# Layer 0 window attention: blocks of 64 queries or keys in two column halves of the array, one bank a head, and a step's value products in one place

## The chip, the cores and the metric

The kernel runs on one core of a Trainium2 chip. The metric is the device time of one execution in microseconds. Three runs of the kernel before took 5398.77 to 5411.32 us, with a median of 5408.9 us.

## The reference, cut to what matters

The program is a two-layer model over 16 sequences of 512 tokens with 256 features. The change touches only the attention of layer 0, in which each query sees its own key and the 64 keys before it, in 16 heads of 16 features:

```python
offsets = jnp.arange(-W, 1)[None, :]                  # W = 64
idx = q_pos + offsets
local_mask = (idx < 0) | (idx >= S_k)
k_win = k[:, :, gidx, :];  v_win = v[:, :, gidx, :]
scores = jnp.einsum('bhqd,bhqwd->bhqw', q, k_win)
scores = jnp.where(mask, -jnp.inf, scores)
m = jnp.max(scores, axis=-1, keepdims=True)
e = jnp.exp(scores - m)
probs = e / jnp.sum(e, axis=-1, keepdims=True)
ctx = jnp.einsum('bhqw,bhqwd->bhqd', probs, v_win)
```

Everything after it (the gate, the full attention of layer 1, the experts) is the same in both kernels.

## The kernel before, in words

The program is a row of stages with a barrier of all engines between them: `project_context`, `window_attention`, `close_window`, `open_full`, `full_attention`, `close_full`, `route`, `experts`. The change is in `window_attention` and in the mask constants of `shape_constants`.

`window_attention` makes 64 steps, one for each sequence and group of four heads. Queries and keys lie in SBUF as stacks of 96 rows of bf16 (`qst`, `kst`, three parts of each number), with three more rows for the shift, that is the negated maximum of a query. A step has two kinds of products:

- *Items* find the maximum. Queries lie on the output's partitions, keys on its columns. In the kernel before an item is one head and two blocks of 128 queries (`MAXJOBS`, eight a step). One matmul of the identity with the constant `outside` (384 columns of bf16) fills the bank with 0 or a large negative number (L789), and two products of 192 or 128 columns are added to it (L794). VectorE takes the maximum along the columns (L754). After the last item of a step it makes the shift in five small operations in a chain, each of which waits for the one before (L759 to L763). The shift is turned by TensorE (the *turn*, L783), copied by VectorE (L749), and sent into row 96 of the query stack by a DMA that ScalarE issues (`send_shift`, L713).
- *Scores* are computed again with keys on the partitions, now with the shift (L805 for the mask, L808 for the products). A head takes two banks, and two heads have their banks at a time. ScalarE takes the exponential of a head in one instruction, 128 partitions by 768 elements (L728). *Values* then multiply the exponentials by the values and a column of ones, in fp32: for each of four blocks of keys the four heads go to partitions 0, 32, 64 and 96 of one bank (L821). ScalarE copies the bank to SBUF (L709), and SyncE stores it (L658).

The order is written out by hand. In window `s`, TensorE does scores of head 0, the first value block of step `s-1`, two items of step `s+3`; scores of head 1, value block 1, the turn of step `s+2` and an item; scores of head 2, value block 2, two items; scores of head 3, value block 3, three items. The turn of step `s+2` needs the chain of small operations behind the last item of step `s+2`, which is the last item of window `s-1`. The items go through three banks in turn. On VectorE the items stand in the same order. ScalarE has the four exponentials, `send_shift` behind the second of them, and the copy of the values at the end. GpSimd places the values of step `s+1` into the padded tile `vaug` once the value products of step `s-1` are done. SyncE loads the stacks five steps ahead (three DMAs for keys, six for queries), and stores the result of the step before. A prologue makes the items of steps 0, 1 and 2 and the turns of steps 0 and 1.

Of the kernel before, what the change touches and what calls it, by code (L numbers as in the profile page):

```python
# [7 lines left out]
ACT = mybir.ActivationFunctionType  # L8
# [545 lines left out]
def window_attention(nc, d):  # L554
# [4 lines left out]
    HQ = GROUP * QT  # L559
    SPAN = P + WINDOW  # L560
# [9 lines left out]
    def window_items(s, left):  # L570
# [9 lines left out]
        at = len(prologue) + PER_WINDOW * (s.k % 3)  # L580
        return [(*it, base + n, (at + n) % 3) for n, it in enumerate(items)]
# [10 lines left out]
    prologue = [(*it, n, n % 3) for n, it in enumerate(prologue)]  # L592
    assert PER_WINDOW % 3 == 0

    with ExitStack() as ctx:
        sp_ = Space(nc, ctx, "win")
        sb, ps = sp_.sb, sp_.ps
        score = [ps(f"score{i}", [P, 2, 512]) for i in range(2)]
        item_bank = [ps(f"item{i}", [P, 512]) for i in range(3)]
        value = ps("value", [P, SQ])  # L600
# [4 lines left out]
        prob = [[sb(f"prob{h}{i}", [P, 2, 2 * SPAN]) for i in range(2)] for h in range(GROUP)]  # L605
# [7 lines left out]
        outside = sb("outside", [P, 2, 2 * SPAN], BF16)  # L613
# [9 lines left out]
        place_start, vaug_done = sem("place_start"), sem("vaug_done")  # L623
# [58 lines left out]
        def _(pool):  # L682
# [4 lines left out]
            pool.wait_ge(pads_set, 4)  # L687

# [16 lines left out]
        def _(act):  # L705
            def read_values(s):
                act.wait_ge(value_done, s.n + 1)
                at_least(act, attn_out[s.par], 16 * half(s))
                nc.scalar.copy(raw[s.par][:, :], value[:, :]).then_inc(value_read, 1)  # L709

# [8 lines left out]
            act.wait_ge(ones_in, 32 * STACKS)  # L719
            for k in range(2):  # L720
                send_shift(Eighth(0, k))

            def window(s, first, left):
                for h in range(GROUP):
# [3 lines left out]
                    nc.scalar.activation(prob[h][s.par][:, :, :], score[h % 2][:, :, 0:2 * SPAN], ACT.Exp,  # L728
# [6 lines left out]
            read_values(Eighth(0, STEPS - 1))  # L735

        @block.vector
        def _(dve):
# [4 lines left out]
            def item(kind, s, j, number, bank):  # L743
                dve.wait_ge(item_full, number + 1)
                if kind == "turn":
# [3 lines left out]
                    nc.vector.tensor_copy(shiftT[s.par][:, :], item_bank[bank][:, :].bitcast(BF16)[:, 0:P]).then_inc(item_read, 1)  # L749
                    return  # L750
                h, qts = MAXJOBS[j]
                hq = h * QT + qts[0]
# [12 lines left out]

            for it in prologue:
                item(*it)

            def window(s, first, left):
                for it in window_items(s, left):  # L770
                    item(*it)
# [2018 lines left out]
```

## Time and profile before

| | |
|---|---|
| runs shown | 5398.77, 5408.9, 5411.32 us |
| profiled execution | 5409.27 us, span 5407.4 us |
| busy share of the span | PE 90%, DVE 72%, ACT 50%, POOL 23% |
| granted TensorE clock, mean | 0.941 |
| items' maxima, L754 | 512 instructions, mean 552 ns, 262.0 us busy |
| exponentials of the scores, L728 | 256 instructions, mean 811 ns, 207.5 us busy |

Times are microseconds from the start of the span. PE is TensorE's matmuls, PEld its weight loads, DVE VectorE, ACT ScalarE, POOL GpSimd, SP SyncE; a q behind an engine is its sequencer. A busy matmul row runs from its start until its last result has landed, so rows that follow each other overlap, and the distance of two starts is what one costs in a stream. The stage of the change runs from about 328.7 us to 825.8 us of the span. The clock is given as a share of 2.4 GHz.

### The profile page before, as it was taken

To read this page: it belongs to the slowest core of one execution; us is meant where nothing else is said; L and a number is where in the kernel's file an instruction comes from. 1 tells how busy PE (TensorE), PEld (TensorE's weight loads), DVE (VectorE), ACT (ScalarE), POOL (GpSimd) and SP (SyncE) were. 2 spreads that over 40 slices of the span, in tenths; PEclk is the share of its full clock that TensorE was granted. 3 is DMA by queue.
4 is the path that set the end of the run, shared out by engine and by line. 5 is a ranking of instruction groups with operands and counts; after the bars stand their busy time and mean duration, and the time that the engine had idled before them with its cause. 6 is when DMAs were issued, how large, how long until landed. Compare 5 with 4: busy or idle time off the path is not lost. (4 is left out here: it accounts for less than half of the span.)

```text
span 5407.4 us, 90976 instructions
## 1 busy us (share of the span) xinstructions
PE 4887.9 (90%) x28783; PEld 2800.2 (52%) x28784; DVE 3896.2 (72%) x7609; ACT 2692.4 (50%) x3563; POOL 1236.4 (23%) x964
## 2 busy tenths in 40 slices
PE   8979997997699999999999999999997911999999
PEld 4546665775244444443444444444432710888887
DVE  7766765664768888887888878888884831787786
ACT  2225552222337777776677767777764100444443
POOL 5620001222611010010010001000000345454454
PEclk9989998998889999999999999999998855999999
DMA  7765654223843323323323333323221654333332
GB/s 218 222 179 163 163 143 120 82 69 100 255 88 74 66 47 69 67 59 75 66 46 72 67 60 74 62 49 71 51 45 49 199 157 157 60 61 81 60 61 36
DMA packets 326812, 519.64 MB, mean 96 GB/s; under 512 B 50000, under 2 KB 242863, under 8 KB 324192
## 3 DMA queue, kind: packets, MB, share of 16 engines
q1 hardware_dynamic: 294816, 461.48, 35.0%
q0 software_dynamic: 28208, 51.82, 4.6%
q8 instruction: 226, 3.70, 0.3%
q14 instruction: 202, 1.65, 0.1%
q10 hardware_dynamic: 3360, 0.98, 0.1%
HBM read 254.97 MB, written 179.55 MB: 80 GB/s over the span
## 5 line engine op out<-in xcount | busy, mean ns | idle before, releaser
L1185 DVE TENSOR_REDUCE full_peak<-full_item 128x1 f32<-128x512 f32 (+2 forms) x3392 | 2035.3, 654 | 467.1 <-PE full_item L1252 461.6
L1155 ACT ACTIVATE full_prob<-full_score 128x1024 f32<-128x1024 f32 (+1 forms) x1792 | 1650.8, 961 | 641.4 <-PE full_score L1263 634.4
L1252 PE MATMUL full_item<-full_kst,full_qst 49*128 49x512 f32 (+1 forms) x4096 | 1204.1, 406 | 36.7 <-DVE full_peak L1185 24.3
L1263 PE MATMUL full_score<-full_qst,full_kst 51*128 51x512 f32 (+1 forms) x3328 | 1110.8, 448 | 21.2 <-ACT full_prob L1155 12.1
L1263 PEld LDWEIGHTS full_score<-full_qst,full_kst 51*128 51x128 f32 (+1 forms) x3328 | 480.5, 183 | 935.9 <-ACT full_prob L1155 602.3
L1277 PE MATMUL full_value<-full_prob,full_vaug 128*17 128x512 f32 x6656 | 886.5, 605 | 0.8 <-ACT full_raw L1142 0.7
L1252 PEld LDWEIGHTS full_item<-full_kst,full_qst 49*128 49x128 f32 x4096 | 630.7, 189 | 180.2 <-DVE full_peak L1185 129.8
L2562 ACT ACTIVATE moe_h<-moe_hbank,moe_b 128x512 f32<-128x512 f32 (+1 forms) x320 | 199.9, 625 | 453.8 <-PE moe_hbank L2655 447.8
L1100 POOL TENSOR_TENSOR full_low<-full_low,full_high 128x1601 f32<-128x1601 f32 x32 | 115.7, 3615 | 1194.3 <-DVE full_high L1171 1194.3
L2665 PE MATMUL moe_ybank<-moe_w_both,moe_h_high 128*128 128x512 f32 x1088 | 386.5, 399 | 0.0
L1096 POOL TENSOR_TENSOR full_low<-full_low,full_keep 128x1601 f32<-128x1601 f32 x32 | 116.0, 3624 | 1068.1 <-ACT full_low L1128 1068.1
L754 DVE TENSOR_REDUCE win_peak<-win_item 128x2 f32<-128x384 f32 x512 | 262.0, 552 | 124.0 <-PE win_item L794 117.1
L728 ACT ACTIVATE win_prob<-win_score 128x768 f32<-128x768 f32 x256 | 207.5, 811 | 266.5 <-PE win_score L808 263.3
L2667 PE MATMUL moe_ybank<-moe_w_both,moe_h_low 128*128 128x256 f32 x1088 | 304.6, 280 | 0.0
L2527 POOL DMA_INDIRECT out<-moe_y,moe_to_token x136 | 234.5, 1724 | 121.7 <-POOL moe_y L2523 86.9
L2653 PE MATMUL moe_hbank<-moe_x_high,moe_w_high 128*128 128x512 f32 (+1 forms) x640 | 236.6, 370 | 17.7 <-DVE moe_x_low L2593 15.7
L1277 PEld LDWEIGHTS full_value<-full_prob,full_vaug 128*17 128x17 f32 x6656 | 110.4, 95 | 246.9 <-issue 223.8
L2523 POOL TENSOR_SCALAR moe_y<-moe_y,moe_weight 128x256 f32<-128x256 f32 x136 | 194.6, 1431 | 190.8 <-issue 110.6
L2655 PE MATMUL moe_hbank<-moe_x_high,moe_w_low 128*128 128x512 f32 (+1 forms) x640 | 236.3, 369 | 0.0
L2654 PE MATMUL moe_hbank<-moe_x_low,moe_w_high 128*128 128x512 f32 (+1 forms) x640 | 235.9, 369 | 0.0
L2665 PEld LDWEIGHTS moe_ybank<-moe_w_both,moe_h_high 128*128 128x128 f32 x1088 | 204.2, 188 | 47.1
L1227 PE MATMUL full_score<-full_ctxT,full_wk 128*128 128x512 f32 (+1 forms) x512 | 218.5, 552 | 4.6 <-DMA full_ctxT<-in_ctxT 3.6
(274 smaller groups left out, 7197.3 us busy)
## 6 DMA issues: line engine op xcount, KB each, us to landing
full_kst<-full_high SPq DMA_DIRECT2D x256, 200.1 KB
full_ctxT<-in_ctxT SPq DMA_DIRECT2D x16, 1601.0 KB, 9.0
full_kst<-full_low SPq DMA_DIRECT2D x128, 200.1 KB
win_qst<-scratch_q SPq DMA_DIRECT2D x384, 64.0 KB, 2.7
full_qst<-scratch_q SPq DMA_DIRECT2D x384, 64.0 KB
scratch_xbuf<-ctxp_zero POOLq DMA_DIRECT2D x17, 1032.0 KB, 7.8
moe_x<-scratch_xbuf SPq DMA_DIRECT2D x32, 516.0 KB, 3.7
scratch_attn<-win_raw SPq DMA_DIRECT2D x64, 256.0 KB, 2.1
```

The costliest lines, as they stand in the source:

```text
L754: nc.vector.tensor_reduce(peak[s.par][:, hq:hq + 2], src, AX, ALU.max).then_inc(item_read, 1)
L1155: nc.scalar.activation(prob[h][(s.par * PAIRS + t) % 2][0:rows, 0:banks, :], score[u % 2][0:rows, 0:banks, :], ACT.Exp, scale=SCALE).then_ ...
L1185: nc.vector.tensor_reduce(peak[s.par][:, hq:hq + len(qts), c], src, AX, ALU.max).then_inc(item_read, 1)
L1252: ins = nc.tensor.matmul(ps[:, at:at + z - a], qst[s.slot][rows, h // 2, qt * P:(qt + 1) * P].bitcast(F32R), kst[s.slot][rows, h // 2, a:z ...
L1263: ins = nc.tensor.matmul(score[u % 2][0:z - a, kt % 2, :], kst[s.slot][rows, h // 2, a:z].bitcast(F32R), qst[s.slot][rows, h // 2, :].bitc ...
L1277: ins = nc.tensor.matmul(value[32 * h:32 * h + VW, :], vaug[batch_par(s)][0:rows, kt, GROUP * s.slot + h, :], src, start=(kt == 0), stop=( ...
L2527: pool.indirect_dma_start(d["out"], bass.IndirectOffsetOnAxis(to_token[pg][:, i:i + 1], 0), y[pg][:, i, :], None, bounds_check=TOKENS + SL ...
L2653: nc.tensor.matmul(out, high, x_high[pg][:, kc, 0:cols], start=(kc == 0), stop=False)
L2654: nc.tensor.matmul(out, high, x_low[pg][:, kc, 0:cols], start=False, stop=False)
L2655: ins = nc.tensor.matmul(out, low, x_high[pg][:, kc, 0:cols], start=False, stop=(kc == KC - 1))
L2665: nc.tensor.matmul(bank[:, :, :], h_high[:, hc, i * P:(i + 1) * P], w2_both[par][:, hc, :, :], start=(hc == 0), stop=False, skip_group_che ...
L2667: ins = nc.tensor.matmul(bank[:, 0, :], h_low[:, hc, i * P:(i + 1) * P], w2_both[par][:, hc, 0, :], start=False, stop=(hc == HC - 1), skip ...
```

## The change

Scores and items work on blocks of 64. An item is now one head (four a step instead of eight), in one bank of 128 partitions by 4 by 128 columns: the queries of a block of 64 lie in the lower or the upper 64 partitions and see 128 keys. Each product has 64 columns of weights and goes to partitions 0 to 63 or 64 to 127, so that the mask takes two matmuls of 512 columns and the head eight products of 128 columns. Scores have the same form, and a head takes one bank instead of two. The exponential of a head takes two ScalarE instructions, one for each half of the partitions, 512 elements each, which write to different columns of a tile `prob` that GpSimd has cleared at the start of the stage (ScalarE waits for this, `prob_set`). There are four item banks instead of three, and two value banks instead of one. All four value blocks of step `s-1` stand in one place, behind the items of head 1. One item instead of two stands ahead of the turn (`AHEAD`). VectorE instead of ScalarE copies the value bank; the copy stands behind the third of the four items.

```diff
-    MAXJOBS = [(h, [qt, qt + 1]) for h in range(GROUP) for qt in (0, 2)]
     UNITS = GROUP
-    NMAX = len(MAXJOBS)
+    NMAX = GROUP
     PER_WINDOW = NMAX + 1
-    AHEAD = 2
+    ITEM_BANKS = 4
+    AHEAD = 1
...
-        score = [ps(f"score{i}", [P, 2, 512]) for i in range(2)]
-        item_bank = [ps(f"item{i}", [P, 512]) for i in range(3)]
-        value = ps("value", [P, SQ])
+        score = [ps(f"score{i}", [P, kts, P]) for i in range(2)]
+        item_bank = [ps(f"item{i}", [P, QT, P]) for i in range(ITEM_BANKS)]
+        value = [ps(f"value{i}", [P, SQ]) for i in range(2)]
...
+            for i in range(2):
+                for h in range(GROUP):
+                    nc.gpsimd.memset(prob[h][i][:, :, :], 0.0).then_inc(prob_set, 1)
...
             act.wait_ge(ones_in, 32 * STACKS)
+            act.wait_ge(prob_set, 2 * GROUP)
...
-                    nc.scalar.activation(prob[h][s.par][:, :, :], score[h % 2][:, :, 0:2 * SPAN], ACT.Exp,
+                    nc.scalar.activation(prob[h][s.par][0:HALF, :, 0:P], score[h % 2][0:HALF, :, :], ACT.Exp, scale=SCALE)
+                    nc.scalar.activation(prob[h][s.par][HALF:P, :, HALF:SPAN], score[h % 2][HALF:P, :, :], ACT.Exp,
                                          scale=SCALE).then_inc(exp_done, 1)
...
-                if not first:
-                    read_values(s.plus(-1))
...
-                nc.vector.tensor_reduce(peak[s.par][:, hq:hq + 2], src, AX, ALU.max).then_inc(item_read, 1)
+                nc.vector.tensor_reduce(peak[s.par][:, j * QT:(j + 1) * QT], item_bank[bank][:, :, :], AX,
+                                        ALU.max).then_inc(item_read, 1)
...
+                nc.vector.tensor_copy(raw[s.par][:, :], value[s.par][:, :]).then_inc(value_read, 1)
+
             def window(s, first, left):
-                for it in window_items(s, left):
+                items = window_items(s, left)
+                for it in items[:4]:
+                    item(*it)
+                if not first:
+                    read_values(s.plus(-1))
+                for it in items[4:]:
                     item(*it)
...
+            def mask(bank, which):
+
+                for half_row in range(2):
+                    m = slice(HALF * half_row, HALF * half_row + HALF)
+                    nc.tensor.matmul(bank[m, :, :].rearrange("p i k -> p (i k)"), ident16[:, m], outside[:, which, :],
+                                     start=True, stop=True)
...
+                mask(ps, 0)
+                for qt in range(QT):
+                    for half_row in range(2):
+                        q = qt * P + half_row * HALF
+                        a, z = max(0, q - WINDOW), q + HALF
+                        ins = nc.tensor.matmul(ps[half_row * HALF:(half_row + 1) * HALF, qt, P - (z - a):P],
+                                               qst[s.slot][0:SHIFT_ROW, j, q:q + HALF], kst[s.slot][0:SHIFT_ROW, j, a:z],
+                                               start=False, stop=True, skip_group_check=True)
                 ins.then_inc(item_full, 1)
...
+                mask(ps, 1)
                 for kt in range(kts):
+                    for half_row in range(2):
+                        k = kt * P + half_row * HALF
+                        z = min(k + P, SQ)
+                        ins = nc.tensor.matmul(ps[half_row * HALF:(half_row + 1) * HALF, kt, 0:z - k],
+                                               kst[s.slot][:, h, k:k + HALF], qst[s.slot][:, h, k:z],
+                                               start=False, stop=True, skip_group_check=True)
                 ins.then_inc(score_full, 1)
...
+            def values(s):
+
+                pe.wait_ge(vaug_done, s.n + 1)
+                at_least(pe, value_read, s.n - 1)
+                pe.wait_ge(exp_done, UNITS * s.n + UNITS)
+                for kt in range(kts):
+                    for h in range(GROUP):
+                        a, z = kt * P, min(kt * P + SPAN, SQ)
+                        ins = nc.tensor.matmul(value[s.par][32 * h:32 * h + 32, a:z], vaug[s.par][:, kt, h, :],
+                                               prob[h][s.par][:, kt, 0:z - a],
+                                               start=(kt == 0), stop=True, skip_group_check=True)
+                ins.then_inc(value_done, 1)
...
+            ITEMS_AFTER = (2, 1, 1, 1)
+            VALUES_AFTER = 1
...
                 for h in range(GROUP):
                     scores(s, h)
-                    if not first:
-                        values(s.plus(-1), h)
-                    due = len(items) * (h + 1) // GROUP
-                    for it in items[given:due]:
+                    for it in items[given:given + ITEMS_AFTER[h]]:
                         item(*it)
-                    given = due
+                    given += ITEMS_AFTER[h]
+                    if h == VALUES_AFTER and not first:
+                        values(s.plus(-1))
```

So a window of TensorE reads: scores 0, item 0, turn; scores 1, item 1, the values of the step before; scores 2, item 2; scores 3, item 3. VectorE has: item 0, the copy of the turn, items 1 and 2, the copy of the values, item 3 with the chain of small operations.

## Rows read from the trace of the kernel before

**Rows 1.** Busy time in stretches; columns: stretch, length, five engines, clock, DMA share, GB/s.
```profile
342.30:360.30 18.00, 13.82 (x74) 9.08 (x74) 14.37 (x35) 0.00 (x0) 0.74 (x2) 0.69 1.06 208
365.00:800.00 435.00, 435.00 (x4823) 274.07 (x4820) 305.32 (x837) 221.43 (x298) 23.75 (x59) 1.00 0.59 160
```

**Rows 2.** One step in order of time; columns: start, us, engine, line, what.
```profile
500.44 0.23 PE L783 MATMUL win_item<-win_ident,win_shift_parts 128*128 128x128 bf16 x1
...
500.50 0.33 PE L789 MATMUL win_item<-win_outside,win_ident 128*128 128x384 bf16 x1
500.50 0.26 PEld L794 LDWEIGHTS win_item<-win_kst,win_qst 96*128 96x128 bf16 x2
500.66 0.30 PE L794 MATMUL win_item<-win_kst,win_qst 96*128 96x128 bf16 x2
...
500.81 0.33 PE L805 MATMUL win_score<-win_outside,win_ident 128*128 128x384 bf16 x1
...
500.96 0.73 ACTq L713 DMA_DIRECT2D win_qst<-win_shiftT  x1
...
501.00 0.56 DVE L754 TENSOR_REDUCE win_peak<-win_item 128x2 f32<-128x384 f32 x1
...
501.30 0.30 PE L808 MATMUL win_score<-win_qst,win_kst 99*128 99x192 bf16 x2
501.53 0.16 PEld L821 LDWEIGHTS win_value<-win_prob,win_vaug 128*32 128x32 f32 x8
501.53 0.53 PE L821 MATMUL win_value<-win_prob,win_vaug 128*32 128x192 f32 x8
...
502.00 0.34 PE L789 MATMUL win_item<-win_outside,win_ident 128*128 128x384 bf16 x1
...
504.27 1.49 DVE L754 TENSOR_REDUCE win_peak<-win_item 128x2 f32<-128x384 f32 x3 [0.71 <-PE win_item L794]
...
506.63 0.17 DVE L763 TENSOR_TENSOR win_shift_parts<-win_shift_rest,win_shift_parts 128x16 bf16<-128x16 f32 x1
...
507.74 0.23 PE L783 MATMUL win_item<-win_ident,win_shift_parts 128*128 128x128 bf16 x1
```

**Rows 3.** Groups by shape, whole span; behind the bar: busy us, mean ns.
```profile
L1263 PEld LDWEIGHTS full_score<-full_qst,full_kst 51*128 51x128 f32 x3072 | 448.3, 187 | 812.0 <-ACT full_prob L1155 478.5 <-issue 318.3
...
L1277 PEld LDWEIGHTS full_value<-full_prob,full_vaug 128*17 128x17 f32 x6144 | 101.9, 95 | 222.2 <-issue 200.2 <-ACT full_prob L1155 15.0 <-ACT full_vaug L1132 5.5
```

**Rows 4.** The last value products and the pause before them, in order of time.
```profile
823.75 1.40 PE L821 MATMUL win_value<-win_prob,win_vaug 128*32 128x192 f32 x32 [1.07 <-ACT win_raw L709]
```

**Rows 5.** Groups of VectorE and ScalarE by shape, whole span, columns as in rows 3.
```profile
L1185 DVE TENSOR_REDUCE full_peak<-full_item 128x1 f32<-128x512 f32 x3072 | 1944.3, 684 | 396.5 <-PE full_item L1252 391.1
...
L2588 DVE TENSOR_SCALAR moe_x_cut<-moe_tbank 128x512 uint32<-128x512 uint32 x64 | 41.0, 681 | 0.0
...
L416 DVE SCALAR_TENSOR_TENSOR ctxp_turned<-ctxp_bank,ctxp_bk,ctxp_cos 128x512 f32<-128x512 f32 x32 | 23.8, 742 | 2.0 <-PE ctxp_bank L478 2.0
...
L1155 ACT ACTIVATE full_prob<-full_score 65x512 f32<-65x512 f32 x256 | 142.4, 591 | 64.8 <-PE full_score L1263 63.5
```

**Rows 6.** The first turn in order of time, behind an idle TensorE.
```profile
348.77 0.17 DVE L763 TENSOR_TENSOR win_shift_parts<-win_shift_rest,win_shift_parts 128x16 bf16<-128x16 f32 x1
...
349.09 0.22 PE L783 MATMUL win_item<-win_ident,win_shift_parts 128*128 128x128 bf16 x1 [1.78 <-DVE win_shift_parts L763]
```

**Rows 7.** SyncE's loads in a step, in order of time.
```profile
498.34 1.26 SPq L647 DMA_DIRECT2D win_kst<-scratch_k  x3
499.70 2.86 SPq L652 DMA_DIRECT2D win_qst<-scratch_q  x6
```

**Rows 8.** Stretches around pauses of TensorE, columns as in rows 1.
```profile
347.10:350.50 3.40, 1.04 (x9) 0.61 (x8) 2.01 (x9) 0.00 (x0) 0.00 (x0) 1.00 1.04 207
350.60:353.90 3.30, 3.30 (x18) 2.22 (x17) 3.08 (x7) 0.00 (x0) 0.00 (x0) 0.50 1.07 216
...
822.10:825.00 2.90, 1.83 (x43) 1.30 (x41) 0.00 (x0) 1.29 (x2) 0.00 (x0) 1.00 0.17 64
```

More of the change, by code:

```diff
@@ L579, in window_items @@
         base = len(prologue) + PER_WINDOW * s.n
-        at = len(prologue) + PER_WINDOW * (s.k % 3)
-        return [(*it, base + n, (at + n) % 3) for n, it in enumerate(items)]
+        at = len(prologue) + PER_WINDOW * s.k
+        return [(*it, base + n, (at + n) % ITEM_BANKS) for n, it in enumerate(items)]
     def turn_number(s):
@@ L591, in window_attention @@
                 + [("max", Eighth(0, 2), j) for j in range(NMAX)])
-    prologue = [(*it, n, n % 3) for n, it in enumerate(prologue)]
-    assert PER_WINDOW % 3 == 0
+    prologue = [(*it, n, n % ITEM_BANKS) for n, it in enumerate(prologue)]
     with ExitStack() as ctx:
@@ L604, in window_attention @@
         vaug = [sb(f"vaug{i}", [P, kts, GROUP, 32]) for i in range(2)]
-        prob = [[sb(f"prob{h}{i}", [P, 2, 2 * SPAN]) for i in range(2)] for h in range(GROUP)]
+        prob = [[sb(f"prob{h}{i}", [P, kts, SPAN]) for i in range(2)] for h in range(GROUP)]
         peak = [sb(f"peak{i}", [P, HQ]) for i in range(2)]
@@ L612, in window_attention @@
         ident16 = sb("ident16", [P, P], BF16)
-        outside = sb("outside", [P, 2, 2 * SPAN], BF16)
+        outside = sb("outside", [P, 2, 4 * P], BF16)
         sem, sems = sp_.sem, sp_.sems
@@ L705, in _ @@
         def _(act):
[L706 to L709, printed above, removed]
             def send_shift(s):
@@ L810, in scores @@
-                ins.then_inc(score_full, 1)
-            def values(s, kt):
-                if kt == 0:
-                    pe.wait_ge(vaug_done, s.n + 1)
-                    at_least(pe, value_read, s.n)
-                    pe.wait_ge(exp_done, UNITS * s.n + UNITS)
-                for h in range(GROUP):
-                    a, z = kt * P, min(kt * P + SPAN, SQ)
-                    src = prob[h][s.par][:, kt // 2, kt % 2 * SPAN:kt % 2 * SPAN + z - a]
-                    ins = nc.tensor.matmul(value[32 * h:32 * h + 32, a:z], vaug[s.par][:, kt, h, :], src,
-                                           start=(kt == 0), stop=True, skip_group_check=True)
-                if kt == kts - 1:
-                    ins.then_inc(value_done, 1)
+                    for half_row in range(2):
[4 more added lines that the diff above has]
+                                               start=False, stop=True, skip_group_check=True)
@@ L834, in window @@
                     scores(s, h)
[L835 to L838 removed]
+                    for it in items[given:given + ITEMS_AFTER[h]]:
                         item(*it)
[L840 removed]
+                    given += ITEMS_AFTER[h]
+                    if h == VALUES_AFTER and not first:
+                        values(s.plus(-1))
             windows_by_eight(pe, window)
[L842 to L843 removed]
+            values(Eighth(0, STEPS - 1))
 def full_attention(nc, d):
@@ L2699, in shape_constants @@
     sin = np.stack([np.sin(ang[:, f % half]) * (-1 if f < half else 1) for f in row]).astype(np.float32)
-    r, c = np.arange(P)[:, None], np.arange(P + WINDOW)[None, :]
     bf16 = mybir.dt.np(BF16)
-    near = np.where((r <= c) & (c <= r + WINDOW), 0.0, OUTSIDE)
-    first = np.where(c < WINDOW, OUTSIDE, near)
-    outside = np.stack([np.concatenate(x, 1) for x in ((first, near), (near, near))], 1).astype(bf16)
+    r, c = np.arange(P)[:, None], np.arange(P)[None, :]
+    near = np.where((r % (P // 2) <= c) & (c <= r % (P // 2) + WINDOW), 0.0, OUTSIDE)
+    first = np.where((r < P // 2) & (c < WINDOW), OUTSIDE, near)
+    last = np.where((r >= P // 2) & (c >= WINDOW), OUTSIDE, near)
+    outside = np.stack([np.concatenate(x, 1) for x in ((first, near, near, near), (near, near, near, last))], 1).astype(bf16)
     before = (r < np.arange(P)[None, :]).astype(bf16)
```

36 lines of the change are left out of this document (10 added, 26 removed).

## The prediction

> **What bounds the kernel now.** I read the stretches first. From 365 to 800 us, nearly the whole of the stage that is changed, PE is busy 435.00 of 435.00 us at clock 1.00 (2.4 GHz), while DVE is at 305.32, ACT at 221.43 and the DMA engines at 0.59 [rows 1]. So the stage goes by TensorE, and no result of it is late. Then one step in order of time [rows 2]: the turn starts at 500.44 and the next at 507.74. The 64 turns run from 349.09 us to 808.98 us, and from the fourth on they are 7.31 us apart. In this step a mask of 384 columns takes from 500.50 to 500.66, which is 384 columns at 2.4 GHz; the two products behind it (128 and 192 columns) end their turn at 500.81. Eight such item blocks and eight score blocks are 16 x 0.32 = 5.1 us. A value block starts at 501.53 and the next work at 502.00. Of these 0.47 us the columns are only 0.32 (192 columns, two instructions a head): about 0.09 go ahead of it (products issued at 501.30 and having 320 columns are through at 501.44) and about 0.10 to 0.15 behind it. Four value blocks cost 3 x 0.47 + 0.36 and 4 x 0.09 = 2.1 us. With the turn that is 7.3 us.
>
> The chain of small operations is hidden now. The last maxima of a step are three in a row, 504.27 to 505.76; the chain ends with L763 at 506.80 [rows 2], and the turn that needs it starts at 507.74. TensorE has 2.8 us of work between the last item and the turn. This cover is what I look at below.
>
> **The change part by part.** All sums are for one step, and go against the profiled execution of 5409.3 us (span 5407.4), which lies 0.4 us from the median of 5408.9 us.
>
> *A unit (mask and products of a head).* Items and scores had 768 + 704 columns a head. Now the mask is 512 columns for each half and the products are 4 x 128 columns for each half. If the halves run side by side, the mask is 512 / 2400 = 0.22 us. Each pair of products is 128 columns, 0.053 us, and some 0.005 for an instruction. Its loads have 64 columns of bf16, a form without a row. fp32 loads have rows of 187 ns at 128 columns and 95 ns at 17 [rows 3], so 0.83 ns a column; two bf16 loads of 128 columns took 0.26 us with the wait between them (at 500.50) [rows 2], about half the fp32 ones each. 64 columns cost between 0.02 us (half of that again) and 0.053 us; I take 0.053, the dearer. That is as long as the product and so still hidden behind it. A unit u is 0.22 + 4 x 0.058 = 0.45 us. There are eight units: 3.6 us, where there were 5.1.
>
> Do the halves run side by side? The value products use four column groups of 32. The last 32 of them ran in 1.40 us [rows 4]; their columns, 2 x 4 x 704 = 5632, would take 2.35 us one after the other at one column a cycle. Eight loads of about 108 ns each began and ended within 0.16 us from 501.53 on [rows 2]; one after the other they would need 8 x 32 x 0.83 = 0.21 us and the tail of the last. So products and loads of different column groups run side by side in the form seen, with 32 columns and fp32. With 64 columns and bf16 no row shows it. The bounds are u = 0.45 (side by side) and u = 0.43 + 8 x 0.058 = 0.90 (nothing side by side); between them is u = 0.22 + 4 x 0.116 = 0.68, where only the loads follow each other. I take 0.45, since the rows of the nearest form show both kinds of overlap.
>
> The Trainium skill ("TensorE: Matmul & The Clock Gate", Part 3, "The mechanism") says that weight loads overlap running matmuls only if the row groups differ; the two halves here have the same rows. The trace differs: loads of L794 start at 500.50, while the mask L789 with the same rows runs until 500.83 [rows 2]. By that rule the loads would be laid bare, u would be near 0.66 and the step slower than before.
>
> *The values in one place.* 1.40 us from the first start to the last end [rows 4], less about 0.07 by which the next work may start ahead of that end, and 0.09 ahead: 1.42 us. Before it was 2.1. The turn now stands between products of 64-column form: 0.06 (500.44 to 500.50) [rows 2] and 0.10 to get out of it, which I take from the value blocks; bounds 0 and 0.15. Together TensorE has 3.6 + 1.42 + 0.16 = 5.2 us of work.
>
> *The chain behind the last item.* Now there are only scores 0 and item 0 between item 3 and the turn, 2u = 0.90 us. Against it stand: result of the item to VectorE 0.19 (next start at 500.81, maximum at 501.00), maximum of 512 elements 0.68 [rows 5], the chain of small operations 505.76 to 506.80, 1.05 [rows 2], and 0.15 from its end (348.94) to the turn (349.09) [rows 6]; 2.07 us. VectorE is also late, because the copy of the value bank stands between the maxima of items 2 and 3. Reading a bank with 512 elements takes 0.68 (L2588) [rows 5]; no row has a plain fp32 copy of this size by VectorE, bounds 0.56 (the maximum of 384 elements, [rows 2]) and 0.74 (another operation of 512 elements, L416 in [rows 5]). Maxima in a row are 0.08 closer than their length (three of 0.55 in 1.49) [rows 2]. So the turn of one step hangs on the turn of the step before by a ring. Turn and way out 0.16; scores 1 and item 1 0.90; values 1.42; scores 2 and item 2 0.90; to VectorE 0.19; maximum 2 0.60; copy 0.60; maximum 3 0.68; small operations 1.05; to the turn 0.15. The sum is 6.65 us, longer than TensorE's 5.2. So TensorE, now never idle, waits 1.4 to 1.5 us at each turn. The ring without the copy (over scores 3 and item 3) is 0.16 + 0.90 + 1.42 + 1.80 + 2.07 = 6.35, a lower bound. In front of the turn only head 0's work stands, so nothing else can fill this wait.
>
> *The others.* ScalarE has 8 x 0.59 (65 x 512 elements [rows 5]) and the DMA issue of 0.73 [rows 2], 5.5 us with its gaps; it loses the copy of 0.58. It stays under 6.65; without that cover it would set the step at 5.5. Exponential 1, `send_shift` and exponential 2 in a row need 1.2 + 0.8 us, and scores 2 come 2.3 us behind scores 1, so it is not late. VectorE's work is 4 x 0.68 + 0.68 + 0.23 + 1.0 = 4.6 us where it was 5.13. SyncE issues the loads in 4.2 us [rows 7], with store and registers 5.5 us, five steps ahead: hidden. The bytes are the same, and the DMA share rises from 0.59 to 0.65. The second value bank takes away a wait that is nearly nothing now. GpSimd clears eight tiles of 768 elements, 6 us by its clear of 512 elements in 0.52 us; ScalarE waits for this ahead of its first shift, which left at 349.67 us, and the clear ends at about 336 us. Hidden, 6 us if it were not.
>
> *The sum.* From 7.31 to 6.65 is 0.66 us; the steady steps are 61: 40 us. The prologue (342.3 to 360.3, [rows 1]) is held by 24 maxima and two chains, partly at the lower clock. Twelve maxima of 0.60 replace 24 of 0.47 to 0.64, about 4 us. The last two steps have no items and go by the exponentials, 4 x 1.2 us a step in both kernels: 0. Forecast 5409.3 - 44 = 5365 us; with 0.06 to 0.30 us a step for the copy and the way out of the turn its own range is 5345 to 5385.
>
> **Rivals.**
> *The weight loads of the two halves do not overlap.* Place: each pair of products; price: 0.116 instead of 0.058, u = 0.68. For it: a load of 64 columns is as long as its product, so there is no room, and no row shows two loads of 64 columns. Against it: the eight loads in 0.16 us. TensorE is then 8 x 0.68 + 1.58 = 7.0 us and waits at the turn for 2.07 - 1.36 = 0.7: 7.7 us. That is slower: 61 x 0.42 = 26, the prologue gives 3, so 5432 us. It decides from u = 0.61 on, where both the ring (4u + 4.85) and TensorE (6u + 3.65) reach 7.3. The skill's rule above would lead here too.
> *Nothing of the halves overlaps.* u = 0.90, a step of 8 x 0.90 + 1.58 + 0.3 = 9.1: 61 x 1.8 = 107, 5515 us. The change would then not do what it says. Against it are rows 4.
> *The ring does not bite*, and the step goes to 5.2 us: 61 x 2.1 + 4 = 133, 5276 us. Nothing in the order allows it, only much shorter small operations than the 0.21 us steps seen.
> *The clock falls.* A pause like the one ahead of the first turn (PE 1.04 of 3.40 us busy) was followed by clock 0.50 [rows 8]; the pause ahead of the last values (1.07 us without a result under way) was not, at 1.83 of 2.90 us busy [rows 4, 8]. A step with 5.2 of 6.65 us of work is nearer to the second. If a third of the time ran at 1.2 GHz, the ring's 3.3 us of TensorE would double there: 6.65 + 1.1 = 7.75, 5435 us.
>
> **How the numbers follow.** A measurement of this kernel tells 0.3% (16 us) from no change. Forecast 0.68; a unit of 0.55 to 0.65, which ends within 0.3%, 0.07; loads one after the other 0.11; nothing side by side 0.04; the clock 0.04; the ring not biting 0.06. Faster is 0.68 + 0.06 = 0.74, same 0.07, slower 0.19. The range from 5335 to 5433 us holds the forecast, the middle and most of the first rival; outside are 0.04 and 0.06 and the rest of the slow cases.
>
> **What would show it.** Right: maxima of 512 elements at 0.68 us, half as many; products of the lower and upper half starting within 0.01 us of each other, pairs 0.058 us apart; one value stretch of 1.4 us; turns 6.6 us apart with about 1.4 us of idle PE ahead of each, ended by the last small operation; the DVE copy directly between two maxima. Wrong: pairs 0.11 us apart, turns closer than 6.3 us, a clock under 1.00 in the steady stretch, or ScalarE or SyncE as what the turn or the scores wait for.

## The result, and the profile after

The changed kernel takes 5380.0 us (median of 5 runs, 5375.6 to 5380.8) where the kernel before takes 5406.3 us (5 runs, 5398.8 to 5411.3): a ratio of 0.9950, with a 95% interval from 0.9936 to 0.9965. That is 26 us faster, and 15 us more than the forecast of 5365. The profiled execution has a span of 5378.0 us and a time of 5379.97 us.

Two stretches of the stage, with the columns of [rows 1]: the prologue, and the steady steps.

```profile
342.30:360.30 18.00, 11.85 (x126) 8.89 (x128) 10.67 (x25) 0.00 (x0) 0.74 (x2) 0.50 1.06 216
365.00:760.00 395.00, 320.08 (x6487) 223.43 (x6483) 241.92 (x631) 272.07 (x461) 22.93 (x57) 0.97 0.63 174
```

TensorE, which had no idle time in this stage [rows 1], is now busy for 81% of it. The clock is no longer 1.00 throughout. One step in order of time, as in [rows 2]:

```profile
500.29 0.41 PE L789 MATMUL win_item<-win_outside,win_ident 128*64 128x512 bf16 x2
500.29 0.44 PEld L807 LDWEIGHTS win_item<-win_kst,win_qst 96*64 96x64 bf16 x8
500.51 0.39 PE L807 MATMUL win_item<-win_kst,win_qst 96*64 96x128 bf16 x8
...
500.73 0.38 PE L789 MATMUL win_score<-win_outside,win_ident 128*64 128x512 bf16 x2
...
500.94 0.69 DVE L749 TENSOR_REDUCE win_peak<-win_item 128x4 f32<-128x512 f32 x1 [1.62 <-PE win_item L807]
...
501.12 0.59 ACT L729 ACTIVATE win_prob<-win_score 64x512 f32<-64x512 f32 x1
...
501.55 0.68 DVE L768 COPY win_raw<-win_value 128x512 f32<-128x512 f32 x1
...
502.14 0.68 DVE L749 TENSOR_REDUCE win_peak<-win_item 128x4 f32<-128x512 f32 x1
...
503.69 0.17 DVE L759 TENSOR_TENSOR win_shift_parts<-win_shift_rest,win_shift_parts 128x16 bf16<-128x16 f32 x1
...
503.93 0.23 PE L797 MATMUL win_item<-win_ident,win_shift_parts 128*128 128x128 bf16 x1 [1.11 <-DVE win_shift_parts L759]
...
505.06 1.40 PE L833 MATMUL win_value<-win_prob,win_vaug 128*32 128x192 f32 x32
```

The reader sees the predicted step. From mask to mask (500.29 to 500.73) a unit, that is the mask and the products of one head, is 0.44 us. The masks of both halves take 0.22 of it and the eight products the other 0.22, or 0.055 us a pair: the two halves run side by side. Maximum, copy and maximum stand directly behind each other on VectorE. The last small operation starts at 503.69, and the turn that waited for it starts at 503.93, behind 1.11 us of idle TensorE. Then the values run in one piece of 1.40 us.

One sign is there that the prediction counted as wrong: the scores of head 0 wait 0.17 us for an exponential in most steps. It costs nothing, since the turn behind them waits for VectorE all the same.

Most turns are 6.55 to 6.63 us apart, where the forecast was 6.65. But ten of the intervals are longer, in pairs. The waits of TensorE's two queues between 400 and 740 us (what waited, for what; total us, times, longest) show two reasons to wait where one was foreseen:

```profile
PEld win_item L797 <- DVE win_shift_parts L759: 53.4, 42, 1.3
PEld win_score L789 <- issue: 25.6, 55, 3.3
...
PE win_score L789 <- issue: 14.7, 5, 3.1
```

"Issue" is a wait for no result of another engine. There are five long ones of some 3 us. The first in order of time:

```profile
464.27 0.39 PE L807 MATMUL win_item<-win_kst,win_qst 96*64 96x128 bf16 x8
467.70 0.64 PE L789 MATMUL win_score<-win_outside,win_ident 128*64 128x512 bf16 x2 [3.05 <-issue]
468.13 0.63 PE L820 MATMUL win_score<-win_qst,win_kst 99*64 99x128 bf16 x8
```

And the stretches around it (columns as before, the clock is the third number from the end):

```profile
457.00:464.40 7.40, 6.28 (x141) 4.46 (x137) 4.76 (x12) 5.57 (x10) 0.40 (x1) 1.00 0.52 157
464.40:467.50 3.10, 0.26 (x10) 0.09 (x5) 2.20 (x8) 1.40 (x3) 0.00 (x0) 1.00 0.43 135
467.50:475.00 7.50, 6.49 (x105) 4.31 (x107) 1.78 (x4) 3.04 (x6) 0.40 (x1) 0.77 0.74 178
```

TensorE stands still for 3 us, and behind the pause part of the work runs at 1.2 GHz: a mask pair takes 0.64 instead of 0.41 us. The turns around the five pauses are 9.23 + 8.22, 8.08 + 8.16, 9.20 + 7.40, 9.08 + 8.46 and 8.78 + 7.50 us apart. That is 84.1 us for ten steps of 6.55, so 18.6 us are lost. The pauses come once in eight steps, where TensorE goes back to the start of its hardware loop (`windows_by_eight`: eight steps written out, a loop over six bodies of eight steps each, eight steps written out). The queue that brings instructions, between 400 and 740 us (packets, MB, share of 16 DMA engines), first before, then after:

```profile
q8 instruction: 7, 0.11, 0.1%
```

```profile
q8 instruction: 53, 0.87, 1.2%
```

Before, the loop's body was fetched once, in its first pass. Now it is fetched again in each pass, 8 packets of about 16 KB in each 50 us.

The 29.3 us between the two profiled executions (5409.27 and 5379.97) are best counted from window to window, by the first mask of head 0's scores. The last turn is no mark for this. In window 61 it has no items beside it, and it stood behind head 3 before (808.98, 4.7 us into the window) and stands behind head 0 now (780.64, 2.2 us into it).

- Prologue, up to window 0 (360.35 before, 359.79 now): 0.6 us gained.
- Window 0, which has no values yet: 5.50 us before, 6.24 now, so 0.7 lost.
- Windows 1 to 60 (up to 804.28 and 778.48): 26.0 us gained. Sixty steps of 6.56 us instead of 7.31 would have given 44.6, and the pauses took 18.6 back.
- From window 61 to the last copy of values (826.15 and 799.86): 21.9 us before, 21.4 now, 0.5 gained.
- Outside the stage 3 us, about as much as single runs of one kernel differ.

### The profile page after: what moved, and what is told of

Read it like the earlier page. It is cut to its first block and busy times, and to the rows that moved or that the text cites. A ratio compares the mean times of both kernels' runs of the same rounds, so it can differ in the third digit from the quotient of the medians.

```text
span 5378.0 us, 94696 instructions
## 1 busy us (share of the span) xinstructions
PE 4779.9 (89%) x30831; PEld 2757.7 (51%) x30832; DVE 3838.0 (71%) x7417; ACT 2757.5 (51%) x3755; POOL 1244.1 (23%) x972
## 5 line engine op out<-in xcount | busy, mean ns | idle before, releaser
L749 DVE TENSOR_REDUCE win_peak<-win_item 128x4 f32<-128x512 f32 x256 | 176.3, 689 | 170.9 <-PE win_item L807 170.6
L728 ACT ACTIVATE win_prob<-win_score 64x512 f32<-64x512 f32 x256 | 151.4, 591 | 171.0 <-PE win_score L820 167.9
```

## The experiments

All are compared with the kernel before, which had medians of 5403.7 to 5404.5 us in them (5406.3 beside the changed kernel). The stages after this one, the same in all kernels, take 4567 to 4584 us in the profiled executions, so the distance of two kernels is also given by the stage itself where it matters. Line numbers are each kernel's own and differ by a few.

### TensorE's steps written out

The theory: the pauses are fetches of a loop body that is too long to be kept. The rival: they come from the data, or from a result that the profile does not show. Only TensorE's program is changed:

```
+def windows_flat(eng, body):
+    for left in range(STEPS - 1, -1, -1):
+        body(Eighth(0, STEPS - 1 - left), left == STEPS - 1, min(left, 8))
...
-            windows_by_eight(pe, window)
+            windows_flat(pe, window)
```

> The changed kernel, but TensorE's 48 middle steps are written out one after the other instead of as a loop of 8 steps that runs 6 times; all other engines keep their loops. In the changed kernel's trace turns are 6.55 us apart except at the five returns of TensorE's loop, where two steps together take 3.1 to 4.4 us more (18.6 us in all), with nothing but instruction fetch (16 KB DMAs that never stop) to wait for. Theory A (the return of the loop lays bare a fetch of instructions, since the body no longer stays in the buffer): the five long pairs go, about 5380 - 18.6 = 5361 us, turns 6.5 to 6.65 us apart everywhere, clock 1.00 in the steady stretch. Theory B (the pauses come from data, such as the loads of values or stacks): they stay, 5380 us.

Measured: 5359.7 us (5 runs, 5354.3 to 5365.4), ratio 0.9921 (0.9908 to 0.9935), 20 us less than the changed kernel. All steady steps are 6.63 us apart, none is long, and the last turn moves from 780.64 to 764.82 us, so 16 of the 20 us lie in this stage. The waits between 400 and 740 us no longer have an issue row of 3 us (compare 3.1 and 3.3 above). The first row is the usual wait at the turn, 1.3 us of its weight load, which the profile here puts down to "issue"; the second shows the same wait with its cause:

```profile
PEld win_item L804 <- issue: 64.2, 52, 1.3
PE win_item L804 <- DVE win_shift_parts L766: 57.4, 52, 1.1
...
PEld win_score L796 <- issue: 22.0, 102, 0.2
```

```profile
365.00:760.00 395.00, 322.50 (x6726) 228.75 (x6730) 251.79 (x658) 282.36 (x479) 23.70 (x59) 1.00 0.66 178
```

The clock is 1.00 again. The instructions still have to be fetched once each (46 packets in the same stretch), but straight on, and with no pause. So the fetch itself is not what costs; the return to the start of the body is.

Written-out steps have a small price of their own, 6.63 us against 6.55 in the loop. Here the last small operation ends at 505.98 and the turn starts at 506.12, 0.15 us later, as in every written-out step:

```profile
505.80 0.18 DVE L766 TENSOR_TENSOR win_shift_parts<-win_shift_rest,win_shift_parts 128x16 bf16<-128x16 f32 x1
...
506.12 0.22 PE L804 MATMUL win_item<-win_ident,win_shift_parts 128*128 128x128 bf16 x1 [1.12 <-DVE win_shift_parts L766]
```

In the loop of the changed kernel it is 0.06 us (503.86 to 503.93), and 0.15 in its own written-out steps at both ends, which are 6.62 to 6.64 us apart. Over the stage this is 2.6 us, and the 18.6 us of the pauses less 2.6 are the 16. Why a written-out turn starts later was not tried.

The same edit in the kernel before is the control: there the body was kept, so nothing should change.

> The kernel before with the same edit as e1. Theory A: before, the fetches of 16 KB stop after the first pass of the loop and the return costs 0.3 us or less, hidden; no change, 5406 us within 3 us, and the fetches now go on to the end of the stage. Theory B says no change as well.

Measured: 5406.1 us, ratio 1.0004 (0.9995 to 1.0013), steps of 7.31 us. The 20 us belong to the changed kernel's longer body, not to loops as such.

A third kernel tells how long is too long. It leaves out the mask products of items and scores (`mask`), so its results are not those of the program. The first product of each half starts the bank in their place, and all products have 128 columns. A step has 32 matmuls and loads less on TensorE. A body of eight steps has 8 x 226 matmuls and loads in the changed kernel, 8 x 194 in this one, and 8 x 162 in the kernel before. The loop is kept.

```
-                mask(ps, 0)
...
-                mask(ps, 1)
```

> The changed kernel with its loop, but without the mask matmuls of scores and items (the first product of each half starts the bank; a masked output is not computed), so that TensorE's loop body shrinks from 226 to 194 loads and matmuls a step, about 116 to 99 KB of 64-byte instructions for 8 steps, where it was 83 KB in the kernel before. The ring loses four masks, 0.9 us, and ScalarE or SyncE hold the step at 5.6 us or more. What is asked is only whether the pauses at the five returns of the loop are still there. Theory A1 (the buffer holds less than 99 KB): pauses of about 3 us and 16 KB fetches all through. Theory A2 (it holds 99 KB but not 116): no pause at the returns, and the fetches end after the first pass.

Measured: 5382.6 us in one run. Between 400 and 740 us there are 8 instruction packets, as good as in the kernel before:

```profile
q8 instruction: 8, 0.13, 0.2%
```

No pause of 3 us is left, so a body of 1552 matmuls and loads is kept and one of 1808 is not. (The other instructions of the body are not in this count.) Yet the kernel is no faster. The first row below is of its windows, the others are of its order of time:

```profile
460.00:560.00 100.00, 72.97 (x1427) 52.98 (x1421) 62.63 (x164) 69.83 (x118) 6.04 (x15) 0.79 0.66 176
```

```profile
563.06 0.39 PE L807 MATMUL win_item<-win_kst,win_qst 96*64 96x128 bf16 x8
...
566.49 0.29 PE L797 MATMUL win_item<-win_ident,win_shift_parts 128*128 128x128 bf16 x1 [1.33 <-DVE win_shift_parts L759]
566.71 0.64 PE L819 MATMUL win_score<-win_qst,win_kst 99*64 99x128 bf16 x8
567.13 0.64 PE L807 MATMUL win_item<-win_kst,win_qst 96*64 96x128 bf16 x8
```

The eight products take 0.39 us ahead of the waits and 0.64 us behind them: the clock falls to 1.2 GHz in most steps, and stands at 0.75 over the steady stretch. Only 16 of the 60 steady steps are undisturbed, 5.73 us in the loop and 5.81 in the written-out steps, and the others are mostly 7.1 to 7.8. (Against 6.55 and 6.63 both are 0.82 us less, 0.205 for each of the four masks on the ring, where a mask was reckoned at 0.22: one more sign that the ring sets the step.) This is the prediction's rival of the falling clock, in another kernel. By the prediction's estimate the changed kernel had 5.2 us of work in 6.6 us, and it kept its clock between the pauses; this one has 5.2 - 8 x 0.22 = 3.4 of 5.73 and did not.

### The turn one item later

If the ring sets the step, then more cover for the chain of small operations must shorten it by as much. Scores and items 0 and 1, four units instead of two, then stand between item 3 and the turn.

```
-    AHEAD = 1
+    AHEAD = 2
...
-            ITEMS_AFTER = (2, 1, 1, 1)
+            ITEMS_AFTER = (1, 2, 1, 1)
```

> The changed kernel with the turn one place later: behind item 1 of its window instead of behind item 0 (AHEAD 2, items 1, 2, 1, 1 after the heads). Theory A (the ring over VectorE holds the step): the ring loses scores 1 and item 1, 0.88 us, and ScalarE's 5.5 us becomes next: a step of 5.7 us where it is 6.55, 61 x 0.85 = 52 us less if the loop returns cost the same, about 5328 us; at most 5345 if they grow. Theory B (TensorE or a load holds the step): no change, 5380.

Measured: 5350.5 us (5340.3 to 5357.1), ratio 0.9898. The undisturbed steps are 5.62 to 5.67 us, as worked out. The time is higher than expected, because the pauses at the returns cost more here (pairs of 10.1 + 6.5 and 10.4 + 6.8 us against twice 5.65, 28 us in all five), and a few other steps are long. The mechanism was right, and the sum missed what stands beside it.

With TensorE's steps written out as well:

> The changed kernel with both edits, the turn behind item 1 (e3) and TensorE's middle steps written out (e1). Theory A: both costs are separate; e3's undisturbed steps of 5.64 us hold everywhere, so e1's 5360 less 61 x 0.99 = 60 us, about 5300 us. In e3's trace scores 0 waited 0.17 us for an exponential and the turn for nothing, so ScalarE's order (two score banks, eight exponentials of 0.59, the DMA issue) is what holds the step now. Theory B (fetching instructions holds every faster step, not just the loop's return): steps over 6 us and 5320 or more.

Measured: 5327.2 us (5324.5 to 5328.5), ratio 0.9854 (0.9840 to 0.9867): 27 us too slow against what was expected. Of the 60 steady intervals 21 are 6.0 to 10.2 us, and half are 5.64 to 5.66. The waits of the matmul queue from 370 to 735 us name a load of queries, which no step of the prediction had as late:

```profile
PE win_item L796 <- DMA win_qst<-scratch_q: 17.6, 14, 3.5
PE win_item L796 <- DVE win_peak L756: 3.1, 7, 0.5
```

SyncE's issues in order of time (start, us, what, how many):

```profile
559.88 3.32 SPq L660 DMA_DIRECT2D win_qst<-scratch_q  x5
563.40 0.37 SPq L666 DMA_DIRECT2D scratch_attn<-win_raw  x1
564.12 1.25 SPq L655 DMA_DIRECT2D win_kst<-scratch_k  x3
565.46 4.35 SPq L660 DMA_DIRECT2D win_qst<-scratch_q  x6
569.99 0.37 SPq L666 DMA_DIRECT2D scratch_attn<-win_raw  x1
```

SyncE hardly rests, and from this store to the next it needs 6.6 us, more than the step of 5.65. The next experiment moves the three key loads of a step to GpSimd's queue, with semaphores of their own; the steps are otherwise those of the last kernel:

```
-                    sp.dma_start(k[at:at + rows, :, :], src[0:rows].rearrange("r (h k) -> r h k", h=GROUP)).then_inc(into, 16)
...
+                if left >= LOADS_AHEAD:
+                    load_keys(pool, s.plus(LOADS_AHEAD))
...
+                    pe.wait_ge(keys_in[s.slot], 16 * 3 * (s.turn + 1))
```

> As e6 (turn behind item 1, TensorE written out), and the three key loads of a step are issued by GpSimd on its own queue, with semaphores of their own, instead of by SyncE. In e6's trace SyncE issues without a pause, 5.7 to 6.6 us a step, and items waited 17.6 us for a query stack; its 23 long steps came to about 30 us. Theory A (SyncE's issues are what lengthens e6's steps): SyncE has 1.8 us less a step, the long steps go, 5.65 us everywhere, 5327 - 28 = 5299 us. Theory B (the DMA engines themselves, at a share of 0.69, are late, or the fetches of instructions): no change, 5327, or slower by GpSimd's dearer issues.

Measured: 5308.4 us (5304.3 to 5317.6), ratio 0.9822 (0.9807 to 0.9837), the fastest kernel of this study. The same waits, in the same stretch:

```profile
PE win_score L804 <- ACT win_prob L744: 7.1, 12, 1.0
PE win_value L849 <- ACT win_prob L744: 2.1, 1, 2.1
PE win_item L812 <- DVE win_shift_parts L774: 1.6, 1, 1.6
```

The wait for the load is gone, all steps but some ten are 5.65 us, and TensorE is busy for 96% of the time between 375 and 700 us. The DMA engines were not the limit: their share is 0.79 in that stretch, higher than before the edit. But the edit takes both issues and bytes from SyncE's queue, so whether its issuing or its one queue was late stays open.

Of the 9 us beyond the expectation, some 4 are in the prologue, where the third turn is at 367.10 us instead of 362.96. Some 2 are in the steps that are still long, and the rest is that the long steps of the kernel before this edit had cost 24.5 us and not 28. The pause of the prologue stands ahead of the second turn, which is at 361.70 us where it was at 355.28:

```profile
356.27 0.64 PE L804 MATMUL win_item<-win_outside,win_ident 128*64 128x512 bf16 x2 [7.42 <-DMA win_qst<-scratch_q]
```

The row names the queries; the keys, which one DMA queue of GpSimd brings now, are the other load of this wait and the one that moved. That they are what came last was not tried by itself.

### The copy of the values

The prediction has the copy in the ring with 0.30 us more than without it (6.65 against 6.35). Two kernels take it out in two ways, both with TensorE's steps written out. In the first the copy stands behind item 3 and the chain:

```
-                for it in items[:4]:
+                for it in items:
                     item(*it)
                 if not first:
                     read_values(s.plus(-1))
-                for it in items[4:]:
-                    item(*it)
```

> The changed kernel with TensorE written out (e1) and VectorE's copy of the value bank behind the last item and its small operations; the turn stays behind item 0. Theory A (the ring goes over item 2, the copy and item 3): item 3 is ready 0.34 us ahead of its maximum in the changed kernel's trace (501.80 against 502.14), so the step goes from 6.63 to 6.29: 61 x 0.34 = 21 us less than e1, 5339 us. Theory B (the turn waits for something else, or the copy costs VectorE its whole length): no change (5360), or 61 x 0.60 = 37 less (5323).

Measured: 5340.2 us (5336.2 to 5341.9), ratio 0.9879, steps of 6.29 us, all but two, just what was worked out. VectorE around the chain, in order of time:

```profile
503.92 0.69 DVE L756 TENSOR_REDUCE win_peak<-win_item 128x4 f32<-128x512 f32 x1 [0.17 <-PE win_item L812]
...
505.48 0.17 DVE L766 TENSOR_TENSOR win_shift_parts<-win_shift_rest,win_shift_parts 128x16 bf16<-128x16 f32 x1
505.57 0.68 DVE L775 COPY win_raw<-win_value 128x512 f32<-128x512 f32 x1
```

The copy now lies in the time in which TensorE does the turn and the scores. In the second, ScalarE copies as in the kernel before (`read_values` back in its program, behind the exponentials of a step):

> As e1, but ScalarE copies the value bank behind its last exponential, as before the change (this part alone undone). Theory A (the copy costs through its place in VectorE's ring): as in e4 the ring goes over item 3 alone, 6.29 us, unless ScalarE, now at 6.1 us a step, delays scores 0 by its copy; so 5340 to 5350 us, faster than e1's 5360. Theory B (moving the copy to VectorE relieved ScalarE, which was near to holding the step): slower than e1, 5375 or more.

Measured: 5345.3 us (5341.5 to 5351.4), ratio 0.9887, steps of 6.30 us. So the copy's move to VectorE, part of the change under study, cost 0.33 us a step. That is some 20 us of steady steps; the stage as a whole ends 16.6 us earlier than with the copy on VectorE, and the median is 14 us lower.

With the turn one item later the expectation was that the ring no longer bites, and so that the copy's place is worth nothing:

> As e6, and VectorE's copy of the value bank moved behind the last item and its small operations. Theory A: with the turn later the ring over VectorE (5.65 less 0.34 at most) is no longer what holds the step, ScalarE is, so the copy's place is worth nothing: as e6 within 5 us, 5300. Theory B (the ring over the copy still holds it at 5.65): 61 x 0.2 to 0.34 = 12 to 20 us less, 5285.

Measured: 5330.6 us (5320.3 to 5332.1), against 5327.2 with the copy in its old place: no difference. But this does not show that the ring had stopped to bite. With the copy in its old place most turns start 0.15 us behind the last small operation, as where the ring holds the step, and the undisturbed step of 5.65 us is the ring's 6.63 less the 0.97 that scores 1 and item 1 take in it (504.09 to 505.06 in the changed kernel's step). With the copy out of the ring the turn has more room, 0.43 to 0.7 us in most steps, and the steps are 5.6 to 5.9 us all the same. So something else, which these runs do not name for certain (loads of queries and exponentials both wait in them), holds the step at nearly the same length.

### The values in one place

The value blocks go back behind each head's scores, four pieces instead of one, and TensorE's steps are written out (which the expectation does not mention; the kernel to compare with is the written-out one, 5359.7 us):

```
                 scores(s, h)
+                if not first:
+                    values(s.plus(-1), [h])
```

> The changed kernel with its value blocks back behind the scores of each head, one at a time, as before (this part alone undone). TensorE has about 0.5 to 0.6 us more to do a step (three more ways in and out of the value form). Theory A (the ring): the ring now goes over three value blocks to the copy, 0.16 + 1.32 + 1.6 + 0.88 + 0.19 + 0.60 + 0.68 + 1.20 = 6.6 us, so a step stays at 6.6 us and the time at 5380 within 6 us: values in one place bring nothing by themselves. Theory B (TensorE's work counts): 61 x 0.55 = 34 us more, 5414 us.

Measured: 5355.3 us (5350.9 to 5358.3), ratio 0.9911. That is no slower than with the values in one place. Steps are 6.57 to 6.68 us, and TensorE waits less at the turn, 0.43 where it was 1.12:

```profile
565.22 0.22 PE L804 MATMUL win_item<-win_ident,win_shift_parts 128*128 128x128 bf16 x1 [0.43 <-DVE win_shift_parts L766]
```

What the single place saves of TensorE's work is lost again as a wait. In this order it brings nothing.

### The order of the halves

Does it matter that products of the lower and the upper half are issued in turns? With TensorE written out, the loops over half and tile are exchanged, so four products of the lower half are issued and then four of the upper:

```
-                for qt in range(QT):
-                    for half_row in range(2):
+                for half_row in range(2):
+                    for qt in range(QT):
```

> As e1, but the eight products of a head are issued as the four of the lower half and then the four of the upper half, instead of lower and upper by turns. Same instructions, same work. Theory A (products of the two halves run side by side only when they follow each other directly): a unit is 0.22 + 7 x 0.058 = 0.63 us or more instead of 0.44, TensorE's work 5.1 + 8 x 0.19 = 6.6, the ring 6.63 + 4 x 0.19 = 7.4, 61 x 0.76 = 46 us more than e1, 5406 us. Theory B (the halves queue on their own, so that the order does not matter, or they never overlapped): 5360 us.

Measured: 5363.6 us (5359.4 to 5368.5), ratio 0.9925 (0.9908 to 0.9941), steps of 6.72 against 6.63 us. A unit, from mask to mask, is 0.44 us as before:

```profile
499.71 0.41 PE L796 MATMUL win_score<-win_outside,win_ident 128*64 128x512 bf16 x2
499.92 0.39 PE L827 MATMUL win_score<-win_qst,win_kst 99*64 99x128 bf16 x8
500.15 0.39 PE L796 MATMUL win_item<-win_outside,win_ident 128*64 128x512 bf16 x2
500.37 0.42 PE L814 MATMUL win_item<-win_kst,win_qst 96*64 96x64 bf16 x8
```

The expectation of serial halves (5406 us) fell. The two halves of the array run side by side even where the products of one are issued four in a row; the last ones end a little later (0.42 against 0.39).

## Why the prediction was right or wrong

**The unit.** Right. 0.45 was forecast, 0.44 measured, with products and weight loads of both halves overlapping. Both rivals with serial halves are refuted. So is, for this kernel, the rule of the Trainium skill that weight loads overlap running matmuls only if the row groups differ ("TensorE: Matmul & The Clock Gate", Part 3, "The mechanism"): the eight loads at 500.29 above run while the mask of the same rows runs from 500.29 to 500.70, and the first products start at 500.51, in time.

**The ring.** Right. 6.65 was forecast, 6.55 to 6.63 measured. A wait of 1.4 to 1.5 us was expected, 1.1 to 1.3 found. Its large terms are as forecast: the values 1.33 us (1.42), the maximum and the copy 0.61 and 0.59 (0.60 each), the small operations 1.04 (1.05). Only the last one, from the small operations to the turn, is 0.06 in the loop instead of 0.15. Other kernels change the ring and move the step by as much: without the copy 6.29 (6.35 forecast), with two more units of cover 5.65 (6.63 less 0.97), without the masks 5.73. The 60 steady steps would have given 44.6 us where 40 were forecast.

**The return of the loop.** The one large term that the sum lacked. The prediction counted what each instruction costs and not that the instructions themselves have to be brought. Two halves need twice as many products and loads, so TensorE's loop body grew from 8 x 162 to 8 x 226. It took back 18.6 us of the 44.6, by pauses and by the slow clock behind them. The time still fell into the forecast's own range of 5345 to 5385, and that is in part luck: the steps gave 5 us more than forecast, and 3 us came from outside the stage. Written out, the kernel came to 5359.7 us.

**The prologue.** Mis-sized: 4 us were forecast, 0.6 gained up to window 0, and lost again in it. VectorE had less to do (10.67 us instead of 14.37), but TensorE ran at clock 0.50 where it had 0.69 [rows 1]. The clock does not explain it all: with the steps written out it was 0.60 in the same stretch, and the third turn came no sooner (361.78 us, against 361.58). What holds the prologue stays open.

**The last steps.** Right. The forecast was 0, by exponentials at 1.2 us a head in both kernels; measured from window 61 on, 0.5 us are gained. Before, a head had one exponential of 0.81 us and a wait of 0.39 for its scores; now it has two of 0.59 without a wait. The heads follow each other 1.20 us apart before and 1.22 now (rows of ScalarE in order of time, before and after):

```profile
816.05 0.81 ACT L728 ACTIVATE win_prob<-win_score 128x768 f32<-128x768 f32 x1 [0.39 <-PE win_score L808]
817.25 0.81 ACT L728 ACTIVATE win_prob<-win_score 128x768 f32<-128x768 f32 x1 [0.39 <-PE win_score L808]
```

```profile
787.17 0.59 ACT L728 ACTIVATE win_prob<-win_score 64x512 f32<-64x512 f32 x1
787.78 0.59 ACT L729 ACTIVATE win_prob<-win_score 64x512 f32<-64x512 f32 x1
788.39 0.59 ACT L728 ACTIVATE win_prob<-win_score 64x512 f32<-64x512 f32 x1
```

ScalarE's 272.07 us of the steady stretch, at 5.5 us a step or less, stay hidden, as forecast.

**SyncE.** Forecast hidden with its 5.5 us a step. True at 6.55. At 5.65 its queue is late, and it is a higher bound than estimated: single rounds of its loads and its store took 6.6 us, with 4.35 for six query loads that took 2.86 before [rows 7]. What slows the issues was not tried.

**The clock.** The rival had the right mechanism for another kernel. The waits at the turn alone did not bring it down (1.00 with the steps written out); the 3 us pauses did.

## What to carry over

When a change turns few wide instructions into many narrow ones inside a hardware loop, count the instructions of the body, and look at the instruction queue's packets for each pass: a body that is no longer kept costs a pause at each return, and the slow clock behind it. When the bound engine gets faster, walk the ring of waits once around to find the step it will fall to, and then every queue that must keep up with this step; here, by medians, the place of the turn was worth 32 us, the returns 20 (16 in the stage), the loads 19 (16 in the stage) and the place of the copy 20 (17 in the stage), beside the 26 of the change itself. These do not add up: with the turn later, the place of the copy was worth nothing. Work taken from the bound engine is worth nothing as long as a ring holds the step.

## What the runs showed of the hardware

- TensorE keeps a loop body of 1552 matmuls and weight loads (8 instruction packets between 400 and 740 us) and fetches one of 1808 again in each pass (53), with some 3 us of pause at each return. Straight code of the same instructions has no pause (46 packets).
- A turn that waits for VectorE starts 0.06 us behind the last small operation inside the loop, and 0.15 us in written-out steps, in the changed kernel as in the one without masks.
- The two halves of 64 columns take their instructions nearly independently: four products of one half issued ahead of four of the other still run side by side (a unit of 0.44 us in both orders).
- Halving the partitions did not shorten a pass of ScalarE, and fewer columns did: an exponential of 64x512 elements took 0.59 us and ScalarE's copy of 128x512 (`L709` before) 0.58, while 128x768 took 0.81.
- TensorE's clock fell in the kernel with less work: the one without masks, whose undisturbed steps are 5.73 us with an estimated 3.4 of work, had a mean clock of 0.75, and the written-out one, with 5.2 in 6.63, had 1.00.
